# Two-layer graph network: edge features transposed while layer 0 runs, one-bank sums from group 40, and node products placed inside the sort

## The reference

```
layer 0, grouped by src:
  h    = relu(x[src] @ W1[:128] + x[dst] @ W1[128:] + b1)
  mask = sigmoid(h @ W2 + b2)
  agg  = seg(mask * x[dst]) / (seg(mask) + 1e-9)
  x1   = LN(x + relu((0.5 x + 0.5 agg, or x where no edge) @ Wl + bl))
layer 1, grouped by dst:
  h    = relu(LN(x1[src] @ Wa + x1[dst] @ Wb + ef @ We + b1) * g + b)
  agg  = seg((h @ W2 + b2) * sigmoid(ef @ gate_w + gate_b))
  out  = LN(x1 + GRU(agg, x1))
```

## Time and profile before

| | us |
|---|---|
| median of 3 runs (4959.86 to 4964.89) | 4959.97 |
| the profiled execution | 4960.52 |
| its span | 4958.7 |
| granted PE clock, mean share of full speed | 0.816 |
| busy: DVE, PE, POOL, ACT | 4011.2, 3225.9, 3223.1, 2376.1 |
| gathers of layer 0, gathers of layer 1 (busy) | 1578.0, 1614.3 |

### The profile page before, as it was taken

How to read it: one execution, slowest core, us unless ns; L and a number is a source line. 1 busy time by engine, 2 the same in 40 slices (tenths; PEclk the granted TensorE clock), 3 DMA queues, 4 the chain that set the end, 5 groups by cost and what they waited for, 6 DMA issues and landing times. The chain is left out here.

```text
span 4958.7 us, 107200 instructions
## 1 busy us (share of the span) xinstructions
PE 3225.9 (65%) x19888; PEld 2878.0 (58%) x19889; DVE 4011.2 (81%) x15190; ACT 2376.1 (48%) x6543; POOL 3223.1 (65%) x3375
## 2 busy tenths in 40 slices
PE   5611266666666666666665677777787877777786
PEld 3511155555555565555554676666676767777775
DVE  7999567777777777777776789888898888888887
ACT  1210023333433434334333566666577777777775
POOL 0000377777777777777774777766677777777774
PEclk9855577778877777777777889888899999999998
DMA  4200344555555555555554444443444444444442
GB/s 128 64 0 0 92 134 136 148 148 149 149 147 149 147 147 149 147 148 149 148 149 107 107 107 110 100 99 97 99 117 116 114 115 116 115 116 114 115 115 68
DMA packets 657188, 579.43 MB, mean 117 GB/s; under 512 B 381874, under 2 KB 522458, under 8 KB 656633
## 3 DMA queue, kind: packets, MB, share of 16 engines
q0 software_dynamic: 133952, 329.07, 24.4%
q1 hardware_dynamic: 523064, 248.60, 19.1%
HBM read 538.53 MB, written 45.05 MB: 118 GB/s over the span
## 5 line engine op out<-in xcount | busy, mean ns | idle before, releaser
L1670 POOL DMA_INDIRECT crows<-c,cols x1664 | 1614.3, 970 | 568.3 <-issue 481.0
L1153 POOL DMA_INDIRECT bxrows<-bx,cols x1664 | 1578.0, 948 | 508.3 <-issue 506.3
L1199 PE MATMUL scattered<-bxrows,hotw 128*128 128x129 f32 x3328 | 691.9, 379 | 617.7 <-DVE hotw L1366 617.3
L1199 PEld LDWEIGHTS scattered<-bxrows,hotw 128*128 128x128 f32 x3328 | 608.0, 275 | 691.8 <-DVE acc L1363 523.0
L1723 PE MATMUL pre<-w1e,efT 128*128 128x129 f32 x3328 | 723.2, 302 | 156.2 <-issue 145.9
L1363 DVE TENSOR_TENSOR acc<-acc,scattered 128x129 f32 x1664 | 467.8, 281 | 327.5 <-ACT mask L1271 323.6
L1725 PE MATMUL pre<-near,hotT 128*128 x3328 | 698.3, 294 | 0.0
L1723 PEld LDWEIGHTS pre<-w1e,efT 128*128 128x128 f32 x3328 | 565.7, 213 | 194.1 <-issue 187.1
L1188 PE MATMUL pre<-near,hotT 128*128 x3328 | 538.2, 328 | 164.1 <-DVE h L1341 131.0
L1188 PEld LDWEIGHTS pre<-near,hotT 128*128 128x128 f32 x3328 | 503.3, 238 | 214.0 <-issue 210.3
L1366 DVE SCALAR_TENSOR_TENSOR hotw<-fixed,cols,mask 128x128 f32<-128x128 f32 x1664 | 573.5, 345 | 2.3 <-ACT mask L1271 2.2
(11 more groups left out here) (260 smaller groups left out, 5989.7 us busy)
## 6 DMA issues: line engine op xcount, KB each, us to landing
spread<-place_rows SPq DMA_DIRECT2D x416, 256.0 KB
ef<-in_edge_attr SPq DMA_DIRECT2D x1664, 32.0 KB
bxrows<-bx,cols POOLq DMA_INDIRECT x1664
crows<-c,cols POOLq DMA_INDIRECT x1664
cols<-columns SPq DMA_DIRECT2D x416, 8.0 KB
x<-x_ SPq DMA_DIRECT2D x98, 64.0 KB
x_turned<-x1T SPq DMA_DIRECT2D x98, 64.0 KB
c<-c_rows SPq DMA_DIRECT2D x98, 64.0 KB
```

Source lines behind the costliest of these rows:

```text
L1153: pool.indirect_dma_start(out=bx[q][:, k, 0:2 * D], out_offset=None, in_=s.bx[:, :], in_offset=bass.IndirectOffsetOnAxis(ap=cols[q][:, 0, ...
L1199: last = nc.tensor.matmul(out[:, bank, at:at + W], hotw[v % 2][:, k, :], bx[v][:, k, D:D + W], start=True, stop=True)
L1670: pool.indirect_dma_start(out=crows[q][:, k, 0:D], out_offset=None, in_=s.c[:, :], in_offset=bass.IndirectOffsetOnAxis(ap=cols[q][:, 0, k: ...
```

## The change

1. **Layer 0 transposes the edge features.** From group 44 on, one block of 1280 edges per group, 157 blocks in all: SP loads it (`load_features`), PE transposes it in five pieces in the third `scattered` bank, ACT copies it to `efT`, SP stores two halves into a table `s.efT` of 64 rows x edges.
2. **Layer 1 loads features from that table**, already transposed, into two buffers instead of four: up to group 75 eight loads of 64 x 128 per group; from group 76 two loads, of eight and of seven steps' columns, at places that the schedule stage computes (`pieces`); the second waits until the first has landed. PE's transposes and ACT's copy go; `w1e` has 64 rows instead of 128.
3. **One-bank sums from group 40** (`THREE`) with up to three tiles, from group 76 (`TWO`) with two, now in both layers. `loop_slots` gets two loops, slots 48 to 75 and 84 to 199, and more slots written out.
4. **The x products lie in the sort**: 28 pairs of tiles before the first "across" level, four before each later one.
5. The schedule stage makes the tiles of steps and the places by transposes on 13 partitions, for both layers; the keys of layer 1 are stored by two transfers instead of four.

The diff, cut to its core:

```diff
+        def share(level):
+
+            cut = [0] + [min(28 + 4 * n, NG + 1) for n in range(7)]
+            return cut[level], cut[level + 1]
...
+THREE, TWO = 40, 76
...
+    def body(o, most=0):
         for q in range(R):
-            steps(o * R + q, q, o, fast=fast)
-            nodes(o * R + q, q, o, fast=fast)
-    body(0, False)
+            steps(o * R + q, q, o, most=most)
+            nodes(o * R + q, q, o)
+    body(0)
     with engine.Fori(1, 4) as o:
         for q in range(R):
             steps(o * R + q, q, o, early=True)
-    for o in range(4, FILL):
-        body(o, False)
-    if early > FILL:
-        with engine.Fori(FILL, early) as o:
-            body(o, False)
-        for o in range(early, early + 2):
-            body(o, False)
-        early += 2
-    with engine.Fori(early, BODIES) as o:
-        body(o, True)
+    for o in range(4, THREE // R + 2):
+        body(o)
+    with engine.Fori(THREE // R + 2, TWO // R) as o:
+        body(o, 3)
+    for o in range(TWO // R, TWO // R + 2):
+        body(o)
+    with engine.Fori(TWO // R + 2, BODIES - 2) as o:
+        body(o, 2)
+    for o in range(BODIES - 2, BODIES):
+        body(o)
     for g in range(GROUPS, last + 1):
         steps(g, g % R, g // R)
         nodes(g, g % R, g // R)
 
 
-def two_sided(g, fast):
-
-
-    return g >= FEW_TILES if isinstance(g, int) else fast
+def most_tiles(g, most):
+
+
+    if isinstance(g, int):
+        return 0 if g < THREE else 3 if g < TWO else 2
+    return most
...
+def ef_group(g, back, most):
+
+
+    i = g - (THREE + 4) - back
+    if isinstance(g, int):
+        return i if 0 <= i < EF_GROUPS else None
+    return i if most else None
...
+                def load_features(g, q, most, features):
+                    i = ef_group(g, 0, most)
+                    if i is None:
+                        return
+                    if not isinstance(i, int) or i >= R:
+                        sp.wait_ge(ef_turned, i * 2 - 6)
+                        sp.sem_inc(sp_go, 1)
+                    if isinstance(i, int) and i == EF_GROUPS - 1:
+                        sp.dma_start(ef[q][0:EF_REST // 5, :, 0, :],
+                                     features[E - EF_REST:E, :].rearrange("(p j) f -> p j f", j=5)).then_inc(ef_in[q], 16)
+                    else:
+                        sp.dma_start(ef[q][:, :, :, :], features[bass.ds(i * TURNED, TURNED), :].rearrange(
+                            "(a p j) f -> p j a f", a=2, j=5)).then_inc(ef_in[q], 16)
+
+                def store_features(g, q, most):
+                    i = ef_group(g, 4, most)
+                    if i is not None:
+                        sp.wait_ge(ef_evac, i * 2 + 2)
+                        sp.sem_inc(sp_go, 1)
+                        for half in range(2):
+                            sp.dma_start(s.efT[:, bass.ds(i * TURNED + half * (TURNED // 2), TURNED // 2)],
+                                         efT[q % 2][half * DE:half * DE + DE, :]).then_inc(ef_out[q % 2], 16)
+
...
+                    folds = most_tiles(g - 1, most) if has(g, 1) else 0
+                    if folds:
+                        places = load_values(nc, mybir.EngineType.PE, in_bank[0:1, bass.ds((g - 1) * G, G)], 2 * W)
+                    if has(g, 0):
+                        i = ef_group(g, 3, most)
+                        if i is not None:
+                            pe.wait_ge(ef_evac, i * 2 + 1)
+                            nc.tensor.transpose(ef_ps[:, 0:P], ef[(q - 3) % R][:, 4, :, :].rearrange("p a f -> p (a f)"),
+                                                s.ident_f[:, :]).then_inc(ef_turned, 1)
                         pe.wait_ge(hotT_made, g + 1)
...
+                        i = ef_group(g, 2, most)
+                        if i is not None:
+                            pe.wait_ge(ef_in[(q - 2) % R], (o - (11 if q >= 2 else 12)) * 16 + 16)
+                            if not isinstance(i, int) or i >= 1:
+                                pe.wait_ge(ef_evac, i * 2)
+                            else:
+                                pe.wait_ge(added, THREE * G)
+                            for j in range(4):
+                                last = nc.tensor.transpose(ef_ps[:, j * P:j * P + P],
+                                                           ef[(q - 2) % R][:, j, :, :].rearrange("p a f -> p (a f)"),
+                                                           s.ident_f[:, :])
+                            last.then_inc(ef_turned, 1)
+                    if folds:
+                        v = (q - 1) % R
+                        pe.wait_ge(added, max(g - 2, THREE) * G if isinstance(g, int) else g * G - 2 * G)
+                        for k in range(G):
+                            if k % 4 == 0:
+                                pe.wait_ge(hotw_made, g * 2 + k // 4 - 1)
+                            there = out[:, v % 2, 0:W] if k == 0 else out[:, v % 2, bass.ds(places[k], W)]
+                            last = nc.tensor.matmul(there, hotw[v % 2][:, k, :], bx[v][:, k, D:D + W],
+                                                    start=(k == 0), stop=(k == G - 1))
+                        last.then_inc(scattered, 3)
+                    elif has(g, 1):
                         v = (q - 1) % R
...
+                        i = ef_group(g, 3, most)
+                        if i is not None:
+                            act.wait_ge(ef_turned, i * 2 + 2)
+                            act.sem_inc(act_go, 1)
+                            nc.scalar.copy(efT[other].rearrange("f (p j) -> f j p", j=5)[:, 4:5, :],
+                                           ef_ps[:, 0:P].rearrange("f (j p) -> f j p", j=1)).then_inc(ef_evac, 1)
...
+                    folds = most_tiles(g - 2, most) if has(g, 2) else 0
+                    adds = has(g, 2) and not folds
+                    if folds:
+                        tiles = load_values(nc, mybir.EngineType.DVE,
+                                            few_tiles[0:1, bass.ds((g - 2) * 3, folds)], TILES + 1)
+                        dve.wait_ge(scattered, (g - 1) * 3)
+                        dve.wait_ge(added, (g - 2) * G)
+                        for place, tile in zip((0, 2 * W, W), tiles):
+                            there = acc[:, bass.ds(tile, 1), 0:W]
+                            dve.tensor_tensor(there, there, out[:, q % 2:q % 2 + 1, place:place + W],
+                                              ALU.add).then_inc(added, G // 2 if folds == 2 else 2 if place == W else 3)
...
-        ef = [sb(f"ef{q}", [P, G, DE], F32) for q in range(R)]
+        efT = [sb(f"efT1_{q}", [DE, (2 * G - 1) * P], F32) for q in range(2)]
...
-
-                def load_features(g, q, features):
-                    edges = load_values(nc, mybir.EngineType.SP, edge_of[0:1, bass.ds(g * G, G)], (E - P) // 64)
+                sp.wait_ge(steps_in, 96)
+
+                def load_features(g, q):
+                    steps_at = load_values(nc, mybir.EngineType.SP, edge_of[0:1, bass.ds(g * G, G)], LAST_CHUNK)
                     for k in range(G):
-                        sp.dma_start(ef[q][:, k, :],
-                                     features[bass.ds(edges[k] * 64, P), :]).then_inc(ef_in[q], 16)
+                        sp.dma_start(efT[q % 2][:, k * P:k * P + P],
+                                     s.efT[:, bass.ds(steps_at[k] * P, P)]).then_inc(ef_in[q], 16)
+
+                def load_first_piece(g, q):
+                    at = load_values(nc, mybir.EngineType.SP, pieces[0:1, bass.ds(g * 3, 1)], CHUNKS - 1)[0]
+                    sp.dma_start(efT[q % 2][:, 0:G * P], s.efT[:, bass.ds(at * P, G * P)]).then_inc(ef_in[q], 16)
+
+                def load_last_piece(g, q, o):
+                    sp.wait_ge(ef_in[q], o * 32 + ef_before + 16)
+                    sp.sem_inc(sp_go, 1)
+                    at = load_values(nc, mybir.EngineType.SP, pieces[0:1, bass.ds(g * 3 + 1, 1)], CHUNKS - 1)[0]
+                    there = load_values(nc, mybir.EngineType.SP, pieces[0:1, bass.ds(g * 3 + 2, 1)], G)[0]
+                    sp.dma_start(efT[q % 2][:, bass.ds(there * P, (G - 1) * P)],
...
+                    if has(g, 1) and (g > TWO if isinstance(g, int) else most == 2):
+                        load_last_piece(g - 1, (q - 1) % R, o - 1 if q == 0 else o)
+                    if has(g, 0) and used(g, R):
...
+                        sp.wait_ge(pre_made, (o - 1) * (3 * R) + 3 * q + 9)
+                        sp.sem_inc(sp_go, 1)
+                        if most_tiles(g, most) == 2:
+                            load_first_piece(g, q)
+                        else:
+                            load_features(g, q)
+                loop_slots(sp, steps, nodes, LAST)
...
-                        pe.wait_ge(ef_in[q], o * (16 * G) + 16 * G)
-                        if used(g, 1):
-                            pe.wait_ge(efT_made, g)
-                        i, t = tile_at(START1, (q - 1) % R, o - (1 if q == 0 else 0), 2)
```

(29 more changed lines are left out.)

447 lines of the change are left out of this document (249 added, 198 removed).

## The result

| | before | after |
|---|---|---|
| median, us (4 runs of each) | 4962.43 | 5150.15 |
| lowest and highest | 4959.86 to 5023.56 | 5085.34 to 5160.4 |
| profiled execution, its span | 4960.52, 4958.7 | 5154.41, 5152.0 |

The changed kernel is slower: the ratio of the means is 1.032, with a 95% interval of 1.0204 to 1.0437. The forecast was 4886 us with a range of 4866 to 4920 us, and faster with 0.88. It was wrong in sign and by 264 us. (e10 deals with the single run of 5023.56 us.)

The account below looks back on a forecast made before the run. DVE was taken to bound the sort and layer 1's groups 40 to 79, POOL everything else in both layers. Terms -65.6 - 6 + 0 + 0 - 3 + 1 - 1 = -74.6 us gave 4886 us, range 4866 to 4920 us.

Parts of the forecast that it names:

- (3) Features in layer 1: Layer 1, features loaded already transposed: PE and ACT work goes, loads arrive in time; 0 us, bound above +66 us.
- The named sign: Layer 1, groups above 76: DVE waiting for PE's pre would show the 0 us for loading transposed features wrong.
- late features: Rival, layer 1 from group 76: the waiting second piece comes too late for PE; 4952 us at 0.5 us per group, chance 0.07.
- (4) Transposes in layer 0: Layer 0 from group 44: added loads, transposes and stores stay hidden; 0 us, bounds -1 and +15 us.
- layer 0 loses POOL's cover: Rival, layer 0: SP's feature load delays the next columns, or DMA is too full; 5043 us at 1 us per group, chance 0.07.
- (1) One-bank sums from group 40: Layer 1, groups 40 to 79: fewer DVE sums let POOL set the pace; -65.6 us, bounds -73.7 and -57 us.
- The rival of the jump back: Layer 1, three-tile loop: DVE still idles at its jump, losing 2 to 8 us; 4888 to 4894 us, chance 0.12.
- (2) Start of layer 1: Layer 1, first four groups: fewer feature loads ahead of the columns restart POOL earlier; -6 us, bounds -8.7 and 0.
- (5) Drain: End of layer 0: last group makes two sums instead of eight; -3 us, between -6 and 0.
- (6) Sort: Sort and schedule: moved products stay hidden, +1 us (0 to +6); schedule work on 13 partitions, -1 us (-3 to +1).
- the better case: Rival of more gained: start, drain and groups 40 to 79 all reach their bounds; 4869 us, chance 0.06.

Follow-up runs that it names:

- e10: Kernel before with only the change's order of x products in the sort; 12 runs from 4964.27 to 4971.43 us, ratio 0.995.
- e1: Changed kernel with layer 1's feature operands made 128 rows tall, the added rows zeros; 4998.07 us.
- e4: Kernel before with every second feature matmul of layer 1 cut from 128 to 64 rows; 5082.83 us.
- e6: Changed kernel with 64-row operands kept, but in each bank all feature matmuls before all hotT matmuls; 4999.52 us.
- e8: e3 with SP reading one feature place instead of eight in layer 1's groups 4 to 15 and 44 to 75, features wrong; 4874.81 us.
- e2: Changed kernel with PE's register load of the places in layer 0 moved after the slot's pre matmuls; 5035.23 us.
- e9: Kernel before with one more register load, of seven values that are used, at the top of PE's slot in layer 0; 4965.05 us, ratio 1.0015.
- e3: Changed kernel with both 128-row feature operands in layer 1 and the late read of the places in layer 0; 4888.48 us, ratio 0.9829.
- e5: e3 with DVE clearing acc before the upper halves of the feature buffers at layer 1's start; 4890.42 us, one run of 10198 us left aside.

## Why the prediction was wrong, and where it was right

**(3) Features in layer 1: the step that failed first.** It said: "Per group the four transposes on PE and ACT's copy go; neither engine is full (...), so this gives nothing." I had listed that `w1e` shrinks from 128 to 64 rows and gave it no price. It costs 2 x 0.19 us per step, 3.1 us per group, more than the 0.60 us that the four transposes gave back, and PE is then the bound: +22.4 and +94.6 us in groups 4 to 39 and 80 to 207, a part of what groups 40 to 79 should have won, and at the start, where PE runs at half clock. e1, e4 and e6 show it. The named sign, DVE waiting for PE's `pre` above group 76, came, but for another reason than late features. SP's side of the count left out the read of eight registers (1.66 us) and took 4.2 us for eight issues that now take 5.3; that is the 13.4 us of groups 48 to 79 (e8).

**(4) Transposes in layer 0: the step that failed second.** It said: "I take 0, with the bounds -1 and +15 us." The count for PE took matmuls and no register loads, though part 3 of the change brings `places` into layer 0. What the first read leaves exposed stood on the page of before, not at PE's matmuls but at its weight loads, 210.3 us with the releaser "issue" (31.1 us of them one wait at the start; 40.0 us from 1500 to 2000 us, 0.8 us per group):
```profile
L1188 PEld LDWEIGHTS pre<-near,hotT 128*128 128x128 f32 x3328 | 503.3, 238 | 214.0 <-issue 210.3
```
In the changed kernel PE was busy for 316 us of 1500 to 2000 us, stood 144.9 us at the reads and waited only 41 us for DVE: 461 of 500 us were its own program. A group took 10.7 us there, and PE set it. The transposes with the read hidden (e2) and the read without the transposes (e9) are free, and together they cost 108.5 us: neither was costed against what the other left. The rival "layer 0 loses POOL's cover" had the place right, SP's feature load that waits for PE's transposes with the next columns behind it, and the 1 us per group that it took as its example is near the 0.7 us that came (108.5/157). It had no reason why the transposes should be late; that was PE's program. The DMA engines, its other reason, were at 0.76 (e2) where the sum had 0.84 to 0.95, and cost nothing. The Trainium skill has a price (Runtime: NRT & Kernel Launch, Instruction fetch mechanics: about 200 ns per register for such a load, on a page that speaks of the registers that the runtime loads from HBM). The kernel's own reads here took 1.92 us for eight, 0.24 us each.

**(1) One-bank sums from group 40.** Right in mechanism. In e3 groups 40 to 79 take 416.9 us: 58.5 us less than before (95.6 + 379.8 = 475.4 us), of 65.6 us forecast. Groups 40 to 47 were better than forecast (82.2 against 88.4 us). Groups 48 to 79 had 334.7 us, not 321.3 us, because of SP; with SP relieved they have 320.9 us. The rival of the jump back is not what held them (e8), though a refetch was not looked for by itself.

**(2) Start of layer 1.** 45.5 us instead of 48.7 us in e3, -3.2 us where I had -6; the size was off, as each feature load takes 0.77 us of SP instead of 0.70, and the second 16 wait. **(5) Drain.** The turnover took 38.6 to 39.8 us in the kernels with the change's layer 0, against 44.0 us: -4 to -5 us for -3. **(6) Sort.** +1 forecast; the profiled sort took 501.0 us against 506.2 us, and in e10, which has part 4 alone, layer 0 began at 595.7 us against 593.3 us before, so part 4 by itself shows no gain in the executions at full clock. The schedule took 88.0 us against 87.1 us, where I had -1. What I missed is its worth at half clock: 62 us in a third of the executions (e10).

**What was luck, and a slip.** That e3 comes out at 4888 us against a forecast of 4886 us is not a proof of each term. By the traces groups 40 to 79 and the start gave 10 us less than forecast (-58.5 and -3.2 us for -65.6 and -6). Sort and schedule (-3.4 for 0), layer 0 (-2.5 for 0), the turnover (-5.0 for -3) and small terms in the rest gave about as much more. The chances have a slip too: the forecast, the loop's rival and the better case add up to 0.82, and "faster" was given 0.88.

## What to carry to other kernels

Cost every matmul by its neighbours as well as its columns: a change of operand height costs at each change, so pad to the common height or group equal heights. Count register loads in the budget of an engine's program, and put them where the array has work queued. An engine's spare time can be spent once: add up all that a change puts on one engine per group before calling any part hidden, and allow for the lower clock.

## What was not expected of the hardware

- A change between a 64-row and a 128-row matmul cost 0.19 us on the average at full clock (0.39 us per 64-row matmul between 128-row ones, e4; 0.37 us per two changes, e6).
- PE's products ran at half clock for 200 us of uninterrupted work in e9 (granted 0.50), in a kernel that in another execution had 0.97 there. What decides it stays open. Where a trace has no record of the clock yet, the column reads 1.00 (e3 before 207 us, with matmuls of 298 ns), so read it together with the time of a matmul.
- A gather of POOL took 5.83 us in e3 and ended 0.9 us after DVE's 10.81 us clearing of acc; with the clearing earlier it was gone (e5). The five gathers before it ran beside the same clearing at 0.94 us. It is the tenth gather in every trace that has it, and in all of them it ended 0.8 to 0.9 us after the clearing did: 5.89 us in e1 and 5.67 us in e8, and 1.69, 1.60 and 1.51 us in the changed kernel, e2 and e6, where the clearing began earlier against the gathers. In the kernel before and in e5 the tenth began 0.8 and 0.7 us before the end of the clearing, as in the changed kernel, and was not held. Why is left open.
